# Softmax attention in layers of 48 rows: ScalarE copies the values' output between the fourth and the fifth exponential of a step

## The reference, cut to what matters

```python
q, k, v = proj(Wq), proj(Wk), proj(Wv)          # of the layer norm of x; B, S, D = 16, 512, 256
q, k = _apply_rope(q, k, cos, sin)
scores = jnp.einsum('bhqd,bhkd->bhqk', q, k) / jnp.sqrt(jnp.float32(dk))
attn = jax.nn.softmax(scores, axis=-1)
out = jnp.einsum('bhqk,bhkd->bhqd', attn, v)
out = out.transpose(0, 2, 1, 3).reshape(B, S, D)
return out @ Wo.T                                # x = x + this
```

## Time and profile before

| what | us |
|---|---|
| runs | 2607.04, 2609.82, 2615.57 (median 2609.82) |
| the profiled execution, its own time | 2595.47 |
| its span | 2593.7 |
| of that, PE busy | 2344.2 |
| DVE busy | 1703.7 |
| ACT busy | 1317.5 |

### The profile page before, as it was taken

The page is one execution under the profiler, slowest core; times in us unless marked ns, Lnnn a source line. Parts: engine busy times, 40 slices in busy tenths (PEclk is TensorE's granted clock), DMA queues, the critical chain, the costliest instruction groups (busy, mean ns, idle before and its releaser), DMA issues. The chain is left out here.

```text
span 2593.7 us, 50928 instructions
## 1 busy us (share of the span) xinstructions
PE 2344.2 (90%) x15846; PEld 1279.7 (49%) x15846; DVE 1703.7 (66%) x4309; ACT 1317.5 (51%) x2741; POOL 1150.6 (44%) x1495
## 2 busy tenths in 40 slices
PE   8996888888888888888998998799999969998997
PEld 5663222233222233225655765466666646655765
DVE  6777788888788888726764332477777756764322
ACT  5664566666666666655532332455555525532322
POOL 7996101011101011103424777577777743424776
PEclk9997799999999999998999999899999998998999
DMA  6664433422432333215595986111111015695886
GB/s 191 212 200 146 112 85 76 100 83 74 103 80 77 98 82 75 59 33 168 193 320 156 244 219 123 39 38 38 38 38 36 22 49 159 208 308 161 226 229 115
DMA packets 286874, 325.25 MB, mean 125 GB/s; under 512 B 30496, under 2 KB 272368, under 8 KB 286704
## 3 DMA queue, kind: packets, MB, share of 16 engines
q1 hardware_dynamic: 252928, 274.22, 35.3%
q0 software_dynamic: 29184, 46.43, 8.9%
q10 hardware_dynamic: 4592, 2.47, 0.4%
HBM read 217.29 MB, written 105.19 MB: 124 GB/s over the span
## 5 line engine op out<-in xcount | busy, mean ns | idle before, releaser
L720 DVE TENSOR_REDUCE a_row_max<-a_ps_m 128x1 f32<-128x512 f32 x1024 | 643.7, 682 | 130.6 <-PE a_ps_m L619 126.6
L780 ACT ACTIVATE a_probs<-a_ps_s 128x512 f32<-128x512 f32 x1024 | 528.2, 610 | 234.4 <-PE a_ps_s L648 234.4
L665 PE MATMUL a_ps_o<-a_probs,a_va 128*32 128x512 f32 x2048 | 274.2, 608 | 0.8 <-ACT a_o_sb L789 0.8
L1760 POOL TENSOR_TENSOR b_spread<-b_decay,held_own_sb 128x512 f32<-128x512 f32 x256 | 267.7, 1078 | 8.6 <-DVE b_weight L1821 8.6
L648 PE MATMUL a_ps_s<-first_qs,first_ks 48*128 48x512 bf16 (+1 forms) x1024 | 143.0, 390 | 37.7 <-ACT a_probs L780 30.5
L648 PE MATMUL a_ps_s<-second 48*128 48x512 bf16 (+1 forms) x1024 | 139.6, 380 | 40.2 <-ACT a_probs L780 32.7
L1821 DVE TENSOR_TENSOR b_weight<-b_ps_s,b_spread 128x512 f32<-128x512 f32 x256 | 163.7, 681 | 9.4 <-PE b_ps_s L1962 9.4
L558 POOL CAST a_high<-a_row_max 128x32 bf16<-128x32 f32 x32 | 6.5, 204 | 352.2 <-DVE a_row_max L720 352.2
L597 POOL DMA_DIRECT2D x<-a_xo x32 | 24.2, 755 | 270.5 <-DVE a_xo L754 268.1
L619 PE MATMUL a_ps_m<-first_ks,first_qs 48*128 48x512 bf16 x512 | 106.7, 413 | 22.5 <-DVE a_row_max L720 22.5
L318 PE MATMUL a_ps_qk<-a_w_qk,a_xnT 128*128 128x512 f32 x256 | 122.0, 600 | 0.0
(11 more groups left out here) (395 smaller groups left out, 5426.9 us busy)
## 6 DMA issues: line engine op xcount, KB each, us to landing
parts<-second SPq DMA_DIRECT2D x16, 1536.0 KB, 6.2
second<-parts SPq DMA_DIRECT2D x384, 64.0 KB, 2.5
rows<-m_early SPq DMA_DIRECT2D x32, 640.0 KB, 3.7
m_early<-x SPq DMA_DIRECT2D x31, 512.0 KB, 4.1
first_qs<-parts SPq DMA_DIRECT2D x192, 64.0 KB, 2.9
first_ks<-parts SPq DMA_DIRECT2D x192, 64.0 KB, 2.3
m_own<-in_L_ffn_w_gate_dram SPq DMA_DIRECT2D x24, 384.0 KB, 4.4
m_own<-in_L_ffn_w_up_dram SPq DMA_DIRECT2D x24, 384.0 KB, 5.3
```

The lines of the kernel that those rows point to most:

```text
L665: last = nc.tensor.matmul(ps_o[VW * j:VW * (j + 1), :], va[n.u][:, t, (h0 + j) * VW:(h0 + j + 1) * VW], probs[:, group % 2, j, t, :], star ...
L720: nc.vector.tensor_reduce(row_max[:, n.k // 4 % 2, t, e, n.p % 4:n.p % 4 + 1], m_bank(name, step)[:], AX.X, ALU.max).then_inc(m_drained, 1)
L780: nc.scalar.activation(probs[:, group % 2, j, t, :], s_bank(name, step)[:], ACT.Exp, scale=DK ** -0.5).then_inc(s_drained, 1)
L1760: nc.gpsimd.tensor_tensor(spread[:, n % 2, heads].rearrange("p h t c -> p (h t) c"), decay[:, n % 3, heads].rearrange("p h (t o) -> p (h t ...
```

## The change

ScalarE's list for a step is written in another order: the copy of the values' output stands between the fourth and the fifth exponential, where it stood between the second and the third. Nothing else is different.

```diff
-            walk_pairs(act, [(L_S, exponentials(0)), (L_S, exponentials(1)), (L_OCOPY, copy_output)]
-                       + [(L_S, exponentials(i)) for i in range(2, 8)] + [(L_ATT[0], copy_att(0)), (L_ATT[1], copy_att(1))])
+            walk_pairs(act, [(L_S, exponentials(i)) for i in range(4)] + [(L_OCOPY, copy_output)]
+                       + [(L_S, exponentials(i)) for i in range(4, 8)] + [(L_ATT[0], copy_att(0)), (L_ATT[1], copy_att(1))])
```

## The result

| | before | after |
|---|---|---|
| runs, us | 2607.04, 2609.82, 2615.57 | 2544.73, 2546.27, 2549.91 |
| median | 2609.82 | 2546.27 |
| profiled execution: time, span | 2595.47, 2593.7 | 2549.91, 2548.2 |

The ratio is 0.9755, with a 95% interval of [0.9725, 0.9786]. The forecast was 2548, within 2538 to 2582.

The account below looks back on a forecast made before the run. TensorE was taken as the bound, with most of its idle time one wait in odd steps; 62 waits by 1.0 us, 62 us off 2609.8, gave about 2548 us, range 2538 to 2582.

Parts of the forecast that it names:

- The stall: Odd step on TensorE: scores(3) waits for exponential 3 behind the copy; the change removes 1.02 us each, 62 times.
- Exponentials 2 and 3 fit into ScalarE's idle time: ScalarE, odd step: four exponentials in a row take 2.07 us, ending 0.6 us before the copy can start; no cost.
- another wait keeps the stall: Rival, 4%: exponential 2 or scores(3) is held by something else, so nothing changes: 2610 us.
- TensorE's side: Odd step, second half: by TensorE's order max6-7 starts 1.17 us after the first max pair, 1.12 us earlier than before.
- VectorE's side: Odd step: max6-7 must await max4's reduction plus a handover, so it starts 0.98 us earlier than before.
- the handover of 0.2 us: Safety allowance of 0.2 us between a VectorE reduction's end and the TensorE matmul needing its bank.
- the sum's 61 to 69: Whole-kernel gain in us: 62 odd steps at 0.98 to 1.12 us each; 62 us was taken.
- Exponentials 4 to 7 behind the copy: ScalarE, odd step: exponential 7 ends with 0.35 us to spare before the even step's scores(1); no cost, small slack.
- VectorE as the bound: Rival, 10%: odd-step reductions at their full 0.68-0.69 us limit the loop; gain only 30 us, so 2580.
- The 5.93 us: VectorE's own pace in an odd step: 4.98 us for eight reductions plus 0.95 for the division and its gaps.
- The total: Whole kernel: 62 us off the median of 2609.8, about 2548 us; worked-out forecast given 80%.
- The slower rival: Rival, 3%: in the loop, late `m_parts` DMAs make TensorE wait and halve its clock; 81 us slower, 2691.

Follow-up runs that it names:

- copy_after_third: Against the kernel before: the copy placed between the third and fourth exponential; median 2569.03 us, ratio 0.987.
- values_first: The changed kernel with TensorE's fourth product of the values put ahead of the turn of the output; 2548.1 us, ratio 0.975 to the kernel before.
- the longer series: The changed kernel, unedited, timed again in more rounds, twice; medians 2531.82 and 2529.4 us, ratios 0.9736 and 0.9728 to the kernel before.
- copy_after_eighth: Against the kernel before: the copy placed behind all eight exponentials; median 2680.23 us, ratio 1.0244.
- copy_after_sixth: Against the kernel before: the copy placed between the sixth and seventh exponential; median 2590.57 us, ratio 0.9919.

## Why the prediction was right

- **The stall.** Right. The 62 waits of scores(3) were the copy and exponentials 2 and 3 behind it. copy_after_third halves them with one exponential moved.
- **Exponentials 2 and 3 fit into ScalarE's idle time.** Right: four in 2.06 us, and no wait for the product of their own step. The rival that another wait keeps the stall is out.
- **TensorE's side and VectorE's side.** The size was a little off here: the step was put at 5.97 us and measured 5.84. TensorE's side (1.12 us) held, VectorE's (0.98) did not bind. The mis-sized term is the handover of 0.2 us from a reduction to the matmul that takes its bank. In the profile after, max4's reduction starts at 727.79 and lasts some 0.68 us, and max6-7 starts at 728.54, 0.07 behind its end, without having waited. In values_first, where max6-7 does wait for it, it is 0.06 (704.52 + 0.68 = 705.20, and 705.26), and the 55 waits of this kind in the trace of before have 0.06 too; the 0.2 could have been read there. With 1.11 us gained an odd step (6.95 - 5.84), 62 steps give 69 us, and the copies' stretch is 69.1 shorter. That is the upper end of the sum's 61 to 69, not the 62 taken.
- **Exponentials 4 to 7 behind the copy.** Right that nothing waits for them at the start of even steps, and that the slack is small. Exponential 7 ends at 728.23 + 2.06 = 730.29 and scores(1) needs its bank at 730.08 + 0.43 = 730.51, 0.22 us later, not 0.35. And 0.4 us more work in front of them costs 11.6 us, where no slack at all would make it 26; the turn of `att` is what it costs them at, which the prediction did not have.
- **VectorE as the bound.** The rival is out for the change, with reductions some 0.62 us apart ((9.95 - 0.68) / 15), as before. The 5.93 us that the prediction gave VectorE as the least for an odd step was too much: the step took 5.84, so the eight reductions and the 0.95 beside them fit into less. The 4.98 us taken for eight was an even step's length, at TensorE's pace. values_first shows how near it is: 0.3 us later on VectorE comes back at TensorE.
- **The total.** 2548 was forecast and 2546.27 measured; that it is so close is luck, since two differences of 6 to 7 us cancel. The gain was under-estimated by 7 us, and the first comparison's 63.6 us is itself some 6 us short of the 69 to 71 that the longer series give. The distance between the profiled execution and the median, which the prediction carried over from before, is no constant either: 14.3 us before, -3.6 after.
- **The slower rival.** Not seen: the clock stayed at 1.00 from 300 to 1000 us, and the waits for `m_parts` stayed at 12.6 us. They are 17, one more than the 16 that the prediction named as a sign against it, but their sum did not grow. The other half of this rival, waits that bring the clock to its lower level, shows in copy_after_eighth, with waits for the copy.

## What to carry to other kernels

In an in-order engine an item that waits holds up everything behind it, so ask of each item behind a waiting one whether it needs what is waited for, and who waits for it: here two exponentials that needed nothing held the banks of the engine that bounds the loop. The right place has two sides. Ahead of the item belongs what other engines need sooner, and the item itself has a deadline of its own: one place later cost 25 us, four places later made the kernel slower than before. Two profiles should be compared by the stage that was changed: here the rest of the program differed by 23.6 us (69.1 - 45.5), a third of the gain, in the first pair.

## What the runs showed that was not expected

- Two expert stages of the same kernel took 189.2 to 200.5 and 188.7 to 202.2 us from first to last gather in three executions, while the attention stage repeated within 1.2 us.
- A reduction's bank was taken by the matmul that waited for it 0.06 us after the reduction's end (values_first); as with the exponentials (0.05 us in the earlier trace rows), that is shorter than the 0.14 us from the modelled end of the values' product to the copy.
- TensorE's granted clock fell to 0.50 beside 15 of the waits of 1.9 to 2.1 us in the loop of copy_after_eighth, which cost some 27 us; beside the waits of 1.1 us at most of copy_after_sixth it stayed at 1.00 from 300 to 1000 us.
- VectorE could start on a turned block 0.69 us after the first of four transposes, where it was free.
